# A drain on GpSimd behind every eighth gather of table rows

## The reference

```
h = tokenizer(x)                       # four Fourier layers, 20x20 modes, width 32, then two dense layers
h = concatenate([h, txt], axis=1)      # 32 sequences of 192 tokens of 64
h = h + rnn(layernorm(h))
h = h + mixture_of_8_experts(layernorm(h))
h = h + attention(layernorm(h))        # 8 heads
h = h + product_key_attention(layernorm(h))
```

```
kv_scores, indices = _pk(x, Wq_pk, pk_keys)            # 16 weights and 16 indices per token and head
k = einsum('bnhk,bnhkd->bnhd', kv_scores, keys_table[ind])
v = einsum('bnhk,bnhkd->bnhd', kv_scores, values_table[ind])
```

## Time and profile before

| | us |
|---|---|
| median of 3 timed runs | 8,802.18 |
| lowest and highest of them | 8,794.76 and 8,821.96 |
| span of the profiled execution, from its first to its last instruction | 12,370.4 |
| PE busy in it | 7,191.2 |
| DVE busy | 5,008.5 |
| ACT busy | 3,309.2 |
| POOL busy | 5,931.2 |

### The profile page before, as it was taken

How to read it: one execution, slowest core, us unless ns; L and a number is a source line. 1 busy time by engine, 2 the same in 40 slices (tenths; PEclk the granted TensorE clock), 3 DMA queues, 4 the chain that set the end, 5 groups by cost and what they waited for, 6 DMA issues and landing times.

```text
span 12370.4 us, 121689 instructions
## 1 busy us (share of the span) xinstructions
PE 7191.2 (58%) x34736; PEld 5456.4 (44%) x34736; DVE 5008.5 (40%) x16213; ACT 3309.2 (27%) x9869; POOL 5931.2 (48%) x6158
## 2 busy tenths in 40 slices
PE   7758665665756657566665756647576565424103
PEld 5456454443545435454354544435454444313102
DVE  1243625345253442524435253352534435352612
ACT  1112222223222232222322223222222223222222
POOL 0044445455454454544445454454545545565663
PEclk7655655555555555555655555555555555555555
DMA  1011111111111111111111111111111111111111
GB/s 27 7 41 37 35 39 41 38 38 41 36 42 40 40 38 37 41 41 39 36 38 45 36 42 38 37 41 40 39 40 41 39 38 41 41 41 39 41 47 28
DMA packets 658255, 472.33 MB, mean 38 GB/s; under 512 B 557990, under 2 KB 558494, under 8 KB 657183
## 3 DMA queue, kind: packets, MB, share of 16 engines
q0 software_dynamic: 196608, 403.05, 12.7%
q1 hardware_dynamic: 460896, 60.59, 3.1%
HBM read 461.04 MB, written 2.10 MB: 37 GB/s over the span
## 4 chain that ended last, share of the span: by engine, by line
PE 29%; another core or an unknown queue 27%; issue 18%; DVE 16%; DVEq 4%; ACT 4%; SPq 1%; DMA 1%; POOL 0%; ACTq 0%; POOLq 0%
PE MM L438 5%; DVE KV L876 3%; PE PB L1134 2%; PE PB L1107 2%; ACT GATH L869 2%; PE PB L1172 2%; PE PB L1148 1%; PE PB L1162 1%; PE PB L1131 1%; PE MM L390 1%; DVEq L851 1%; DVE I L814 1%; PE MM L453 1%; DVE PF L852 1%
## 5 line engine op out<-in xcount | busy, mean ns | idle before, releaser
L645 POOL DMA_INDIRECT GATH<-in_table,IDX x6144 | 5925.4, 964 | 6313.4 <-DVE KV L876 3824.1
L869 ACT ACTIVATE GATH<-GATH,WT 128x128 f32<-128x128 f32 x6144 | 1907.1, 392 | 237.8 <-issue 236.8
L438 PE MATMUL MM<-SPEC,SW 128*128 128x8 f32 (+1 forms) x8800 | 1259.7, 297 | 863.1 <-issue 420.6
L876 DVE TENSOR_REDUCE KV<-GATH 128x128 f32<-128x2048 f32 x384 | 1391.0, 3622 | 691.7 <-ACT GATH L869 354.1
L438 PEld LDWEIGHTS MM<-SPEC,SW 128*128 128x128 f32 (+1 forms) x8800 | 1266.8, 264 | 864.4 <-issue 862.5
L506 ACT ACTIVATE U<-MM 128x320 f32<-128x320 f32 (+1 forms) x416 | 219.1, 527 | 1882.2 <-remote 988.1
L547 DVE COPY TURN<-TP 80x512 f32<-80x512 f32 (+1 forms) x512 | 347.1, 684 | 925.4 <-remote 391.8
L390 PE MATMUL MM<-F,TURN 128*128 128x80 f32 x2048 | 436.7, 384 | 464.7 <-DVE TURN L547 345.9
L506 ACT ACTIVATE SPEC<-MM 128x160 f32<-128x160 f32 x320 | 96.1, 300 | 2068.2 <-remote 1283.4
L390 PEld LDWEIGHTS MM<-F,TURN 128*128 128x128 f32 x2048 | 404.5, 292 | 535.1 <-issue 278.6
L477 PEld LDWEIGHTS MM<-G,TURN 80*128 80x128 f32 x2048 | 343.5, 240 | 507.1 <-DVE TURN L547 239.0
(11 more groups left out here) (202 smaller groups left out, 11494.3 us busy)
## 6 DMA issues: line engine op xcount, KB each, us to landing
GATH<-in_table,IDX POOLq DMA_INDIRECT x6144
SW<-in_sw SPq DMA_DIRECT2D x1280, 40.0 KB
CONV<-in_cwb SPq DMA_DIRECT2D x128, 4.0 KB
CONV<-in_cwb SPq DMA_DIRECT2D x128, 0.1 KB
U<-in_xT SPq DMA_DIRECT2D x16, 96.0 KB
out<-OUTB SPq DMA_DIRECT2D x16, 96.0 KB
W1E<-in_w SPq DMA_DIRECT2D x1, 520.0 KB
W2E<-in_w SPq DMA_DIRECT2D x1, 512.0 KB
```

Of the source, the lines that this page charges most:

```text
L438: m = e.matmul(pv[r, :, k, :], SW[r, half, k % HM, w:w + WID * beside], Sv[r, :, c * MODES + k, :], start=True, stop=True)
L645: e.indirect_dma_start(GATH[:, r, k, :], None, table, bass.IndirectOffsetOnAxis(IDX[:, u // H, u % H, k:k + 1], 0)).then_inc(gath[r], 16)
L869: m = e.activation(GATH[:, r, k, :], GATH[:, r, k, :], ACT.Copy, scale=WT[:, u // H, u % H, k:k + 1])
L876: e.tensor_reduce(KV[:, u // H, u % H, :], GATH[:, u % RING, :, :].rearrange("p k d -> p d k"), AX.X, ALU.add).then_inc(S["gather_free"], 1)
```

## The change

One line is added in `pool_gather`. Behind the eighth and the sixteenth gather of each unit stands a drain on POOL: it completes when what the engine has begun is complete, and the next gathers are behind it in the program. Nothing else is changed or moved, on any engine.

More of the change, by code:

```diff
@@ L645, in pool_gather @@
                     e.indirect_dma_start(GATH[:, r, k, :], None, table, bass.IndirectOffsetOnAxis(IDX[:, u // H, u % H, k:k + 1], 0)).then_inc(gath[r], 16)
+                    if k % 8 == 7: e.drain()
         def bc(ap, n):
```

## The result

| | before | with the drains |
|---|---|---|
| median of the timed runs, us | 8,798.47 (4 runs) | 10,462.36 (4 runs, 10,457.73 to 10,468.07) |
| ratio, 95% interval | | 1.1887 (1.1862 to 1.1912) |
| span of the profiled execution, us | 12,370.4 | 10,466.2 |
| POOL busy, us | 5,931.2 | 5,940.9 |

The change costs 1,664 us, 18.9%. The first thing to see is the third row: the profiled execution of the drained kernel is as long as its timed runs, while that of the kernel before was 3,572 us over the median of its timed runs.

A forecast was written before the change was run, and what follows sets the result against it. The prediction took POOL to bound the timed kernel, with a path of 8,642 us; 768 drains at 1.8 us add 1,382, giving 10,024, taken as 10,000 us. Its own range was 9,500 to 10,700, widened to 9,150 to 11,000.

The forecast's parts named there:

- The engine that paces: Timed runs go at POOL's pace: its path without waits is 8,642 us, with some 160 us to spare.
- The landing: Behind a drained gather's record, the bytes were taken to land 1.28 us after the record's end.
- The restart: On POOL behind a drain, starting the next gather with an empty queue was taken as 0.80 us.
- The term that failed: Each drain on POOL adds landing plus restart less the usual gap, 1.75 us, taken as 1.8; 768 make 1,382 us.
- The upper bound: Each drain priced like the program's last on POOL, 5.33 us behind the record: 5.83 us, 4,477 us in all.
- The cover: A unit's second drain, hidden in buffer waits in 327 profiled units, has no such cover in timed runs.
- 1 (another engine paces): Another engine, PE at 92% of a round, paces timed runs; drains show only in the last three rounds: 9,100 us; chance 0.12.
- 2 (the last drain's price): Each drain on POOL costs what the program's last one did: 13,120 us or part, 11,000 to 13,000; chance 0.10.
- 3 (descriptors alone): Drains wait only for descriptors and cost the restart, 0.5 us each, 384 us in all: 9,180 us; chance 0.06.
- 4: The drain on POOL returns at once, as if it were not there: 8,810 us; chance 0.04.
- 5 (descriptors made faster with an empty queue): Gathers on POOL are made more quickly with the queue emptied every eight: faster, 8,341 us if gaps vanished; chance 0.02.
- The profile after: Expected span 12,400 to 12,800 us, gaps about 2.1 us before each unit's ninth gather, POOL busy unchanged at 5,925 us.

The follow-up runs named there:

- e5: The kernel before the change, unedited, profiled a second time; 8,805.78 us, with a profiled span of 8,804.0 us.
- e1: Against the drained kernel, each drain replaced by a POOL wait on the buffer's own semaphore until the gathers have landed; 10,366.33 us, ratio 1.1768.
- e2: Against the kernel before, one drain per unit, behind the sixteenth gather, 384 in all; 9,756.52 us, ratio 1.1078.
- e3: Against the kernel before, a drain behind every fourth gather, 1,536 in all; 12,071.89 us, ratio 1.3704.
- e6: Against the kernel before, fourteen gathers per unit instead of sixteen, without the drains; 8,613.35 us, ratio 0.9795.
- e7: Against the kernel before, twelve gathers per unit instead of sixteen, without the drains; 8,480.52 us, ratio 0.9655.
- e4: Against the drained kernel, two drains in a row at each place instead of one; 10,569.53 us, ratio 1.1997.

## Why the prediction was right, and where not

**The engine that paces.** Right, and it carried the forecast. The path of 8,642 us was read from the stretched profile by leaving the waits out; e5 gives 645.1 + 5,961.1 (the gathers) + 1,860.4 (issue without the start) + about 20 + 98 = 8,584, and 8,804 - 239 + 19 = 8,584 from the other side. The 160 us to spare were 220 in waits and 253 in all. With 8,642 the estimate was 58 too high, at most 0.7%.

**The landing.** Taken as 1.28 us; 1.19 at the median. **The restart.** Taken as 0.80; 0.82 at the median and 0.87 in the mean. Both right, but for the 15 pair ends: they take some 2.8 us more each, 43 us in all, and no term of the sum had them.

**The term that failed** is "A drain adds 1.25 + 0.80 - 0.30". It lets the drain end with the last byte. 0.70 us are missing between the two, 768 x 0.70 = 538 us. Of these 0.37 fit the time until a landing is known to POOL's sequencer (0.36 in e1), and 0.33 are what the drain takes for eight gathers, 0.041 us for each since the last (e2, e3). With it the cost is 2.43 us at the median and 2.50 in the mean, 1,917 us against 1,382; less the spare 253 that is the 1,664 measured. The forecast of 10,000 was 462 us low, inside its own range of 9,500 to 10,700.

**The upper bound** of 5.83 us from the program's last drain was a true price, and I set it aside for two reasons. The first, that it ended in a stretch held up by the recording, was wrong: e5 has the same 20.14 us in an execution that was not held up. The second, that it stands behind thousands of gathers and not eight, was right. One good reason would have called for a price between the two: the row had 4.0 us behind the last byte for many gathers, so something was to be expected for eight.

**The cover.** Right: the second drain of a unit had nothing to hide in; the waits for buffers fell from 239 to 11 us.

**The rivals.** 1 (another engine paces) is out by e6, but the limit behind POOL is only 320 us away, so the rival was worth its chance: its sum gave PE 92% of a round, and the chain of e7 is mostly PE. 2 (the last drain's price) is out by the gap of 2.71 us. 3 (descriptors alone) is out by e1 and by the drains' ends behind the last byte. 4 is out. What the Trainium skill states in VectorE: DVE Perf Modes, section The DRAIN you can't avoid, about 12 ns for a framing DRAIN on every engine, doesn't hold for POOL behind gathers: the program's last drain takes 20.1 us in the kernel before. With nothing in flight it takes 53 ns in the drained kernel, and the second drains of e4 take 41 ns. A drain of the change takes 8.5 us by its row and 2.4 us by its effect. 5 (descriptors made faster with an empty queue) is out: 966 ns mean against 964, and 0.30 us between gathers as before.

**The profile after.** I expected a span of 12,400 to 12,800 us. It was 10,466. I took the stretching as a property of recording this kernel; e5 shows the same kernel recorded without it. Gaps of 2.1 us were expected, 2.7 came. POOL's busy time was as expected.

## What to carry to other kernels

A drain on GpSimd behind gathers is a full stop, not a marker: it cost 2.4 us here after eight gathers and about 6 us after sixty-four, against 1.25 us for a gather, and a wait on the gathers' own semaphore is no way round it. Whether that costs anything depends on how long the engine waits for others in an execution of normal length: 239 us of 8,804 here, while its busy share of 68% looked harmless. Compare the span of a profile with the timed median before its waits are believed; if it is longer, look for an engine whose distances did not change.

## What was not expected of the hardware

- A POOL drain takes time for gathers that landed long ago: with 4, 8, 16, 64 and 384 gathers since the last drain it ends 0.53, 0.70, 1.02, 4.04 and 4.05 us behind the last byte. With 4 to 16 its end moves with the last byte; with 64 and 384 it stands at 5.28 to 5.31 us behind the last record, whenever the last byte comes.
- POOL's sequencer runs far ahead of the making of descriptors: the program's last drain begins with twelve gathers of 1.25 us still to be made. A drain takes this lead away. Inside a pair the restart then is 0.73 to 0.96 us; at a pair's end, where 0.305 us stand in e5, it is 3.6 to 3.9 us.
- A profiled execution can be 40% longer than the same kernel's timed runs once and equal to them another time. In the long one the gathers kept their 1.25 us.
